# A new written order of instructions and twelve more filler pieces on TensorE

## The reference

```python
# layer 0, per batch of 256 tokens
xn = layernorm(x)
x = x + attention(xn)        # 16 query heads of 8 features, 4 key/value heads, softmax over 256 keys, Wo + bo
      + experts(xn)          # reduces to: (gate1 + gate2) * relu(xn @ w1) @ w2, gates from softmax(xn @ Wg), two largest
# layer 1, all 2048 tokens
xn = layernorm(x)
x = x + ssm(xn)              # x, z = split(xn @ W_in); conv over 4 taps; silu; dt = softplus(xs @ W_dt + b)
                             # h = h * exp(-exp(A) * dt) + xs @ W_x, 16 states, a scan over the 256 tokens
                             # y = (sum of h + D * xs) * silu(z); y @ W_out
      + ffn(xn)              # silu(w1 x) * (w2 x), then 512x512 gelu, 512x512 gelu, 512->128
```

## Time and profile before

| | us |
|---|---|
| median of three runs | 365.15 |
| the profiled execution | 365.17 |
| its span, first to last instruction | 363.4 |
| TensorE matmul busy | 354.0 |
| VectorE busy | 304.1 |
| ScalarE busy | 303.9 |
| GpSimd busy | 231.9 |

### The profile page before, as it was taken

The page is one execution under the profiler, slowest core; times in us unless marked ns, Lnnn a source line. Parts: engine busy times, 40 slices in busy tenths (PEclk is TensorE's granted clock), DMA queues, the critical chain, the costliest instruction groups (busy, mean ns, idle before and its releaser), DMA issues.

```text
span 363.4 us, 5743 instructions
## 1 busy us (share of the span) xinstructions
PE 354.0 (97%) x1754; PEld 180.2 (50%) x1754; DVE 304.1 (84%) x514; ACT 303.9 (84%) x526; POOL 231.9 (64%) x293
## 2 busy tenths in 40 slices
PE   7989999999999999999989999999999999999996
PEld 5556444657564532533234447444447444554546
DVE  4998988989797777399889768999989989899950
ACT  5865977768599987799989889999899999899930
POOL 2465632334350301328899757999989999999990
PEclk9999999999999999999999999999999999999999
DMA  6265973972922200000000000010000000000000
GB/s 222 60 187 125 183 168 105 267 134 63 240 66 54 60 3 3 22 0 14 11 0 0 4 0 0 2 51 2 0 2 22 29 0 4 0 0 1 2 29 29
DMA packets 29662, 19.62 MB, mean 54 GB/s; under 512 B 4256, under 2 KB 28608, under 8 KB 29376
## 3 DMA queue, kind: packets, MB, share of 16 engines
q1 hardware_dynamic: 29632, 19.26, 21.8%
HBM read 13.69 MB, written 5.37 MB: 52 GB/s over the span
## 4 chain that ended last, share of the span: by engine, by line
PE 87%; ACT 5%; DVE 5%; issue 2%; DVEq 0%; ACTq 0%
PE bank L983 15%; PE bank L971 14%; PE bank L421 7%; PE bank L408 5%; PE bank L960 4%; PE bank L390 4%; PE bank L1054 4%; PE bank L445 4%; PE bank L961 4%; PE bank L1007 4%; PE bank L453 4%; PE bank L944 4%; PE bank L1027 3%; PE bank L1044 2%; ACT pt L614 2%
## 5 line engine op out<-in xcount | busy, mean ns | idle before, releaser
L1295 POOL TENSOR_TENSOR acc<-acc,hb 128x512 f32<-128x512 f32 x128 | 158.2, 1271 | 19.2 <-DVE hb L1239 19.2
L1239 DVE TENSOR_TENSOR_SCAN hb<-da,bank 128x512 f32<-128x512 f32 x128 | 145.9, 1200 | 7.7 <-PE bank L944 6.6
L655 DVE TENSOR_REDUCE mx<-bank 128x2 f32<-128x512 f32 x128 | 81.7, 681 | 10.1 <-PE bank L390 9.3
L1162 ACT ACTIVATE da<-dt,nega 128x510 f32<-128x510 f32 x128 | 82.0, 712 | 0.2
L971 PE MATMUL bank<-sil,ld 128*128 128x512 f32 x128 | 59.1, 594 | 0.4 <-ACT gelu L1143 0.4
L983 PE MATMUL bank<-gelu,ld 128*128 128x512 f32 x128 | 58.4, 593 | 0.0
L614 ACT ACTIVATE pt<-bank 128x512 f32<-128x512 f32 x72 | 39.5, 602 | 2.9 <-PE bank L408 2.2
L408 PE MATMUL bank<-q_st,k_st 51*128 51x512 bf16 x128 | 40.4, 382 | 1.1 <-ACT pt L614 0.8
L390 PE MATMUL bank<-k_st,q_st 48*128 48x256 bf16 x240 | 37.5, 272 | 0.7 <-DVE mx L655 0.4
L983 PEld LDWEIGHTS bank<-gelu,ld 128*128 128x128 f32 x128 | 23.8, 190 | 26.4 <-issue 26.0
L971 PEld LDWEIGHTS bank<-sil,ld 128*128 128x128 f32 x128 | 23.7, 190 | 26.3 <-issue 25.7
(11 more groups left out here) (156 smaller groups left out, 564.3 us busy)
## 6 DMA issues: line engine op xcount, KB each, us to landing
q_st<-q_scr SPq DMA_DIRECT2D x8, 384.0 KB, 5.1
q_st<-q_scr SPq DMA_DIRECT2D x15, 192.0 KB, 3.8
ld<-in_pack SPq DMA_DIRECT2D x2, 1024.0 KB, 8.1
q_scr<-qk_parts SPq DMA_DIRECT2D x8, 192.0 KB, 2.4
k_st<-k_scr SPq DMA_DIRECT2D x15, 96.0 KB, 4.8
q_scr<-qk_parts SPq DMA_DIRECT2D x8, 128.0 KB, 2.0
out<-x SPq DMA_DIRECT2D x8, 128.0 KB, 1.9
ld<-in_pack SPq DMA_DIRECT2D x1, 968.0 KB, 6.1
```

Source lines behind the costliest of these rows:

```text
L655: eng.tensor_reduce(mx[:, 2 * pair:2 * pair + 2, q], score_bank(b, n)[:, :].rearrange("p (h k) -> p h k", h=2), AX.X, ALU.max).then_inc(mx ...
L1162: act(da(n)[:, :, 1:T], dt[:, g % 2, c, :].rearrange("p (b n) -> p b n", b=GB)[:, :, 1:T], ACT.Exp, scale=nega[:, c, s:s + 1]).then_inc(da ...
L1239: eng.tensor_tensor_scan(hb[:, s % NPAIR, c, :], da(n).rearrange("p b n -> p (b n)"), b_bank(g, s)[:, :], 0.0, ALU.mult, ALU.add).then_inc ...
L1295: TT(acc[:, g % 2, c, :], acc[:, g % 2, c, :], hb[:, s % NPAIR, c, :], ALU.add).then_inc(add_ok, 1)
```

## The change

Only the order strings and `NWARM` change. No piece is added or removed on any engine except `warm` on TensorE, of which there are 28 in place of 16; no function changes. The pieces that the text below speaks of, in the order strings of before (-) and after (+), each cut to the stretch that matters; the numbers are those of the pieces, counted from 0:

```diff
# whole lines of the change
-NWARM = 16
+NWARM = 28
# tensor, start: as in the file, numbers written out
-    10*warm xn_transposes0 2*warm project0 warm ffn_in0 project_keys0 warm v_gate0 S0 xn_transposes1 S1
-    xn_transposes2 ffn_in1 xn_transposes3 warm S2 project_keys1 project1 S3 .. S7 xn_transposes4 S8 S9 S10 ffn_out0
-    ... S18 v_gate1 warm S19 ... A0 S23 xn_transposes7 A1 S24 S25 A2 project_keys2 S26
+    11*warm xn_transposes0 3*warm project0 warm ffn_in0 warm project_keys0 warm v_gate0 2*warm S0 xn_transposes1
+    ffn_in1 xn_transposes2 S1 2*warm xn_transposes3 S2 project_keys1 project1 S3 .. S7 2*warm S8 S9 S10
+    xn_transposes4 ffn_out0 ... S18 2*warm v_gate1 S19 ... A0 S22 A1 S23 S24 3*warm xn_transposes7 A2 S25
# tensor, around the end of layer 0
-    A127 proj_out6 b8 pv31 b9 second4 b10 second5 heads7 second6 back7 second7 b11 b12 proj_out7 third0
+    A127 proj_out6 pv31 b8 b9 second4 heads7 second5 b10 second6 back7 second7 b11 proj_out7 b12 third0
# sync
-    x_in0 x_in1 head0 constants0 ffn_weights x_in2 put_keys0 put_keys1 put_keys2 put0 put1 put2 fetch0
-    ... put6 rows0 rows1 rows2 put7 put8 loads0 fetch2 ... stack2 rows6 rows7 rows8 loads1 fetch4
+    x_in0 head0 x_in1 ffn_weights constants0 put0 x_in2 put_keys0 put1 put_keys1 put_keys2 put2 fetch0
+    ... rows0 put6 rows1 rows2 put7 put8 fetch2 loads0 ... loads1 stack2 rows6 rows7 put_keys8 rows8 put15 fetch4
# scalar, start and around the end of layer 0
-    deviation0 roots normalised0 deviation0 xn_out0 normalised1 q_out0 wide_out own_keys0 k_out0
-    ... E127 gelu0 gelu1 D23 D24 o_out7 dt2 dt3 gelu2 gelu3
+    deviation0 roots normalised0 xn_out0 deviation0 q_out0 wide_out normalised1 own_keys0 k_out0
+    ... E127 gelu0 o_out7 gelu1 D23 D24 dt2 dt3 gelu2 gelu3
# vector, start and around the end of layer 0
-    clear_values0 ones moments0 inverse0 moments1 clear_values1 inverse1 first_split0 v_out0 first_split1 M0
-    clear_values2 M1 moments2 M2 M3 inverse2 M4 M5 M6 M7 M8 gate_sum0 clear0 M9 gate_norm0 M10 gated0 M11
-    ... scan7 scan8 clear2 residual6 scan9 heads7
+    ones moments0 clear_values0 inverse0 moments1 inverse1 first_split0 v_out0 first_split1 M0
+    moments2 M1 inverse2 M2 M3 clear_values1 M4 clear_values2 M5 M6 M7 gate_sum0 M8 M9 gate_norm0 M10 gated0 M11
+    ... scan7 residual6 clear2 scan8 heads7
# gpsimd, start
-    ones G0 biased0 biased1 split_k0 split_q0 G1 .. G7 biased2 split_q1 maxima_split0
+    biased0 biased1 G0 ones split_k0 split_q0 G1 .. G7 split_q1 maxima_split0
+    ... split_q3 split_k1 maxima_split2 biased2 split_q4
```

More of the change, by code:

```diff
@@ L72 @@
 ORDERS = dict(
[L73 to L123, removed]
+    sync="""x_in head x_in ffn_weights constants0 put x_in put_keys put 2*put_keys put fetch 2*put_keys put put_keys
+        2*put fetch stack rows put 2*rows 2*put fetch loads stack 2*put rows put put_keys 2*rows fetch 2*put put_keys
+        put loads stack 2*rows put_keys rows put fetch stack 2*rows put rows loads put fetch 3*put stack fetch 2*rows
+        put 3*rows put rows stack put fetch stack 3*rows stack loads 3*rows 2*b_rows out b_rows 2*out b_rows 5*out
+        landed""",
@@ new lines @@
+    tensor="""11*warm xn_transposes 3*warm project warm ffn_in warm project_keys warm v_gate 2*warm S xn_transposes
+        ffn_in xn_transposes S 2*warm xn_transposes S project_keys project 5*S 2*warm 3*S xn_transposes ffn_out
+        project 3*S ffn_in 2*S xn_transposes ffn_in max_rows 3*S 2*warm v_gate 3*S xn_transposes ffn_out A S A 2*S
+        3*warm xn_transposes A S A S A S project_keys A S A S A 2*S project 2*A S A 2*S max_rows ffn_in v_gate A S A S
+        ffn_in A S A S project ffn_out A S A S A S 2*pv A S A S A S pv A S pv A S A S project heads A S A S A S
+        max_rows pv v_gate A S A S A S pv A S A S pv back pv A S A S A S heads proj_out 2*A S A S ffn_in A S A S back
+        ffn_in A S A proj_out ffn_out max_rows A S A S A S pv v_gate A S A S A S 3*pv S A S A S A heads A 2*S project
+        ffn_in A S A S back ffn_in A 2*S A S proj_out ffn_out max_rows A S A S A S project ffn_in A 2*S A S v_gate A S
+        A S ffn_in v_gate S A 2*S ffn_out A S A S A S 4*pv A S A S A S heads A max_rows A S A S back ffn_in A S
+        proj_out ffn_in 2*A S A S ffn_out A S A S A S 3*pv S A S pv S 2*A S A S heads A S A S A back 2*A proj_out 2*A
+        S A S max_rows ffn_in A S v_gate 2*S ffn_in A S x_transposes A S A S ffn_out A S 2*A S 3*pv A S A S pv A S A S
+        A heads A S A S x_in A ffn 3*A pv 2*A max_rows ffn x_in 2*pv x_in A pv A x_in wx ffn 2*step_in back A heads
+        x_transposes ffn b A 2*x_in A pv proj_out A b second x_in 2*second b A wx x_in A b step_in A pv b A step_in A
+        b A second A b A pv A back b A proj_out pv 2*b second heads second b second back second b proj_out b third b
+        2*third b third b 3*third x_transposes third 2*x_in 2*ffn x_in 2*b x_in 2*ffn 2*out b 2*out b out wx out
+        2*second b second b second b second step_in b second b second b second step_in 2*b third x_transposes third
+        x_in b x_in third 2*b 3*third x_in third 2*b third x_in 2*ffn 2*b 2*ffn 3*out second b second wx b second out
+        b out b 3*second b out second b second b step_in b step_in b 2*third b third b third b third b third b 2*third
+        b 2*ffn b 2*ffn b out b 2*second b out b second out b second b second b 2*second b second out b out third b
+        third b out third b third b 4*third 6*out""",
@@ new lines @@
+    vector="""ones moments clear_values inverse moments inverse first_split v_out first_split M moments M inverse 2*M
+        clear_values M clear_values 3*M gate_sum 2*M gate_norm M gated 8*M v_out 2*M gate_sum M gate_norm 10*M gated
+        2*M v_out 4*M gate_sum M gate_norm gated 7*M clear_values 2*M heads 6*M v_out 2*M back_out 2*M heads 2*M
+        gate_sum residual M back_out gate_norm 3*M residual gated 4*M v_out 4*M heads 2*M gate_sum 3*M back_out 2*M
+        gate_norm M residual gated 5*M v_out 3*M gate_sum M gate_norm 2*M gated v_out 2*M gate_sum 3*M heads gate_norm
+        M back_out 2*M residual 2*M statistics M gated 5*M inverse1 2*M heads M back_out 2*M residual 3*M v_out 3*M
+        gate_sum 2*M gate_norm gated 8*M heads conv mul xm mul conv zm xm zm mul clear back_out clear heads scan mul
+        2*conv scan zm scan residual scan zm 3*scan back_out scan residual clear scan heads 2*scan back_out scan
+        residual scan statistics 2*scan inverse1 scan 2*conv 2*mul 2*zm 2*scan 2*mul 3*scan residual1 scan residual1
+        8*scan conv scan conv 2*scan 2*mul 2*zm 2*mul 7*scan residual1 scan residual1 9*scan 2*mul scan 2*mul 13*scan
+        4*residual1""",
@@ L124 @@
+    gpsimd="""2*biased G ones split_k split_q 7*G split_q maxima_split 8*G split_q G maxima_split 7*G split_q split_k
+        maxima_split biased split_q 8*G maxima_split 6*G split_q 2*G maxima_split split_q 15*G maxima_split G
+        constants shifted G maxima_split 7*G maxima_split start split start 7*add split 2*start 22*add shifted 3*add
+        2*y start 8*add start 5*add split 19*add 2*y 3*add split 25*add start 2*add start add y 2*add y 31*add 2*y""",
 )
```

12 lines of the change are left out of this document (added).

## The result

| | before | after |
|---|---|---|
| median of 4 runs, us | 365.16 (365.04 to 365.73) | 374.48 (373.77 to 376.0) |
| ratio, 95% interval | | 1.026 (1.022 to 1.029) |
| the profiled execution | 365.17 | 373.3 |
| its span | 363.4 | 371.5 |

I had forecast 363.8 us, a range of 362.4 to 366.4, and 26% for slower. The sign was wrong.

The account below looks back on a forecast made before the run. TensorE, busy 354.0 of 363.4 us, was taken as the bound as a whole. Fillers ahead of `project0` +0.1, front -0.7 and 150 to 190 us -0.8 gave -1.4: 365.15 to 363.8 us, range 362.4 to 366.4.

Parts of the forecast that it names:

- Elsewhere: Mainly from 190 us on: same TensorE work, no idle, moved neighbours free unless they make a wait; no change counted.
- the gain present at 195 us and absent at the last `out`: A named sign of being wrong: time won by 195 us no longer there at the kernel's last `out`.
- The tail slack of 0.83 us: At the tail, `y` ends 0.83 us before `out`; beyond that, TensorE's gain counts only if GpSimd's sums come earlier.
- The fillers: Twelve more pieces, 24 matmuls, from the start to 41 us: hidden in TensorE's waits, cost 0.
- rival +1.5: Fillers on TensorE's path between 13 and 41 us delay all later scores: +1.5 us, 366.7; chance 0.18.
- VectorE up to 41 us: Up to 41 us: earlier `nmr` gains 1.59, `clear_values1` costs 0.45, `clear0` leaves 0.07; sum 1.21 us gained, 0.7 taken.
- net 0, bounds -0.84 and +0.84: Early front: moved `biased0` and `biased1` slow `first_split0`'s casts and speed `first_split1`'s equally; 0 us, within 0.84 either way.
- The loads: Early transfers: `cst` at 7.9 us, covered by 0.1; `x_in2` near 12.5, in time for `moments2`; late landing could cost 1.0.
- 150 to 190: ScalarE's stage: `o_out7` earlier removes the 0.89 us stall at `heads7`; 0.8 us passes, bounds 0 and 1.1.
- The 1.4 for both: A sign of being right: `third0`, after the 150 to 190 stage, starts 1.4 us or more earlier.
- the front's share: The part won up to 41 us: 0.7 us taken, where VectorE allows 1.21.
- gains given back: Rival: ScalarE at 150 to 190 us or the 0.83 us tail slack takes back most of 0.7; 365.0, chance 0.18.

Follow-up runs that it names:

- e12: The kernel before with only the twelve added fillers in the changed kernel's places (28 in all); 366.2 us, ratio 1.002.
- e16: e1 with GpSimd's memset `ones` put back in front of `biased0`, away from `first_split1`; 364.4 us, ratio 0.996.
- e1: All order strings of the changed kernel up to a cut near 195 us, those of the kernel before behind it; 364.6 us, ratio 0.994.
- e6: The changed kernel with TensorE's `b26` to `b32` moved earlier, between `third8` to `third12`; 377.4 us, ratio 1.031.
- e7: e6 with GpSimd's `start6` and `start7` also moved behind `add65` and `split3` behind `add70`; 370.9 us, ratio 1.014.
- e17: e7 with VectorE's `conv6` and `conv7` also moved behind `scan31` and `scan32`; 373.6 us, ratio 1.019.
- e11: The changed kernel with `start6`, `start7` behind `add65`, `split3` behind `add70`, `start5`, `split2` behind `start4`, and `wx2`, `b_in2` earlier; 370.1 us, ratio 1.010.

## Why the prediction was wrong, point by point

**What fails is the paragraph "Elsewhere".** It says that from 190 us on "moved neighbours cost nothing unless they make a wait", and of GpSimd: "They have 13.3 us idle in 165 and are fed through `b` and `scan`, so I let it pass". Both halves were in my rows, and I never looked where the 13.3 us lie. 9.4 of them lie before 230 us, much of it in the wait for the first inputs of a group (4.0 us at 216.7); from 283 us on GpSimd has 0.8 us idle in 40. Between 230 and 283 us its idle went from 1.6 us to 10.7. `start6`, `start7` and `split3` are three of few pieces whose place decides whether such a wait is filled. Moving the starts out of it costs their 2.1 us, placing split3 ahead of its input 4.4: 6.4 of the 8.6 us by which add127 ends later. The rest belongs to the stretch between 245 and 280 us, where no single piece was found. I had listed only moves "by one to a few positions", and start6 had moved behind 26 of the sums. The sign of being wrong that I had named, "the gain present at 195 us and absent at the last `out`", came true.

**The tail slack of 0.83 us** The earlier trace rows was the right number and pointed the wrong way: I used it as a limit of what can be won. It is also all that GpSimd may be late.

**The fillers** (0 forecast, rival +1.5): right, in this order. TensorE is busy 27.60 us of 28.10 between 13.2 and 41.3, forecast 27.7, idle 0.5. The eleventh at the start is paid for. In the old order they cost 1.1 us at the 29th maximum and 1.0 at the end (e12), so the rival's mechanism exists.

**VectorE up to 41 us** (1.21 forecast, 0.7 to pass): the third `nmr` takes 0.17 us at 17.41 as forecast, the 32nd maximum starts at 39.75 against 40.25: 0.5 in place of 0.7 to 1.2. The term of this sum that failed is first_split "net 0, bounds -0.84 and +0.84". Summed over both casts and both subtractions it went from 0.29 + 0.43 + 0.73 + 0.83 = 2.28 us to 0.45 + 0.84 + 1.80 + 0.41 = 3.50, so +1.2, outside my bounds; the cast alone was 1.5 too slow. Only 0.56 us of it reached the first maximum (13.80 against 13.24), in part because `first_split0` had started 0.39 us earlier. With the memset moved away, in e16, the 32nd maximum starts at 39.30, 0.95 before the kernel before: inside the forecast. I had weighed the memset against the second input of the subtraction; its 0.41 us settle nothing, since it started at 13.45, with the memset done. The cast has one input and was held until then: 11.61 + 1.80 = 13.41 against 11.44 + 1.84 = 13.28. By the Trainium skill (SBUF, "Who interferes with whom") casts can enter a mode that takes the port pair shared with GpSimd; whichever of the two comes first then keeps it, and the other blocks fully. This trace agrees, the memset having started 0.17 us before the cast, and that sentence stood beside the one I used.

**The loads**: q_out0 waited 0.53 us for cst and started at 7.68 us (8.07 before), so cst landed ahead of the forecast 7.9. `x_in2`, issued at 8.62, took 3.6 us to land, near the forecast 12.5 and ahead of `moments2` at 14.40. Nothing was lost.

**150 to 190**: the stall ahead of heads7 is gone, as forecast; o_out7 runs at 184.45 and heads7 at 186.49, and third0 starts at 193.66 against 194.43. That is 0.8 earlier, and the 128th maximum, at 131.94, was 0.1 earlier: this stage gave 0.65 of its forecast 0.8. The 1.4 for both fails by the front's share: of the 0.5 us won at the 32nd maximum only 0.1 is left at the 128th. The rows for `o_out7` and `gelu3` of the kernel after:

```profile
184.45 0.59 ACT L550 ACTIVATE o_sb<-bank 128x512 f32<-128x512 f32 x1
...
192.15 1.27 ACT L1144 ACTIVATE gelu<-bank,ld 128x512 f32<-128x512 f32 x2
```

e1, whose early half is the same, is 0.5 us ahead at its last sum (351.26 against 351.77).

**The rivals**: "gains given back" named ScalarE or the tail slack and priced itself at what is won; none of them allowed that a later stage could lose more than the early ones win. My range ended at 366.4 because every slower rival was an early one and the late loss had no price; that the measured time lies above it owes nothing to the early terms, which came out near their forecast. The late half of the strings, where I had no idle to win, held all the risk, and I gave it no rival.

## What to carry to other kernels

An engine at 92% of a stage can be as much a bound as the one at 100%, if its idle sits in one place: ask for its idle in finer windows, and which pieces fill it. In a written order a piece without a successor nearby (here the product that starts an accumulator) is worth most where its engine would wait, and a piece that waits for another engine should stand behind work that is ready. When strings of several engines change together, join the two versions at cuts where all engines have done the same pieces: five such runs placed the loss, while four moves of my own (e6, e7, e17, e11) only turned one wait into another.
